# Local attention: probabilities multiplied by their reciprocal sums on GpSimd, statistics later, new orders

## What is computed

```python
def _layer(x, wqkv, qs, ksc, wo, lg, lb, w1, b1, w2, b2):
    h = shift_token(x)                    # half of the channels come from the token before
    q, k, v = split(h @ wqkv)             # 8 heads of 64
    q = l2norm(q) * qs;  k = l2norm(k) * ksc
    q, k = rotary_xpos(q, k)
    o = local_attention(q, k, v)          # windows of 64 tokens, keys of this window and the one before
    x = x + o @ wo
    h = layernorm(shift_token(x)) * lg + lb
    a, g = split(h @ w1 + b1)
    return x + (a * gelu(g)) @ w2 + b2
```

## Time and profile before

| | |
|---|---|
| median of 3 runs | 2002.58 us (1999.52 to 2009.76) |
| the profiled execution | 2001.32 us, its span 1999.5 us |
| mean granted TensorE clock | 0.924 |
| busy: PE, DVE, ACT, POOL | 1614.6, 1371.7, 1116.0, 453.6 us |
| the two pairs | about 614 to 1111 us and 1478 to 1977 us of the span, 32 steps of some 31 us |

### The profile page before, as it was taken

One profiled execution on the slowest core, in us unless ns is written; L12 is line 12 of the kernel. 1 busy time (PEld: TensorE's weight loads), 2 busy tenths in 40 slices (PEclk: granted clock), 3 DMA queues, 4 the chain that ended last, 5 costly groups with the idle time before them and its releaser, 6 DMA issues.

```text
span 1999.5 us, 31315 instructions
## 1 busy us (share of the span) xinstructions
PE 1614.6 (81%) x9756; PEld 1271.6 (64%) x9787; DVE 1371.7 (69%) x3495; ACT 1116.0 (56%) x2975; POOL 453.6 (23%) x342
## 2 busy tenths in 40 slices
PE   6999989666466787888887899999967788888886
PEld 5888887344354565666666687777735666666665
DVE  4678768788956768677786466456656867768673
ACT  2354454332124777778777644434236777777774
POOL 1210010000003334343343100000023334334340
PEclk9999999676678999999999999989979999999998
DMA  4000000000010000000000000000000000000000
GB/s 136 1 1 0 0 0 1 0 1 0 0 53 1 3 3 1 3 2 3 3 1 3 2 1 0 0 0 0 1 0 3 2 3 1 3 3 2 3 1 24
DMA packets 15110, 13.49 MB, mean 7 GB/s; under 512 B 11286, under 2 KB 14266, under 8 KB 14650
## 3 DMA queue, kind: packets, MB, share of 16 engines
q1 hardware_dynamic: 15034, 12.55, 2.0%
HBM read 9.41 MB, written 1.05 MB: 5 GB/s over the span
## 4 chain that ended last, share of the span: by engine, by line
PE 50%; DVE 25%; issue 10%; ACT 7%; DMA 5%; SPq 1%; DVEq 1%; POOL 1%; ACTq 0%; POOLq 0%
DVE prob L1027 5%; DMA HS<-XH 5%; PE bank L1739 4%; PE bank L1680 4%; PE bank L1751 4%; PE bank L1700 3%; PE bank L1879 3%; DVE arena_ffn L984 3%; PE bank L1772 3%; DVE arena_ffn L980 2%; ACT prob L1437 2%; DVE nmaxF L717 2%; PE bank L1883 2%; PE bank L1691 2%; PE bank L1899 2%
## 5 line engine op out<-in xcount | busy, mean ns | idle before, releaser
L556 POOL TENSOR_TENSOR arena_ffn<-arena_ffn 128x1024 f32<-128x1024 f32 x60 | 140.9, 2348 | 434.2 <-DVE arena_ffn L984 434.2
L552 POOL TENSOR_TENSOR inv<-ssq,mhalf 128x16 f32<-128x16 f32 x64 | 188.3, 2942 | 160.6 <-DVE ssq L993 160.6
L1437 ACT ACTIVATE prob<-bank,nmaxF 128x128 f32<-128x128 f32 x512 | 180.9, 372 | 65.7 <-DVE nmaxF L717 65.7
L1751 PE MATMUL bank<-packF,hT 128*128 128x512 f32 x256 | 146.7, 702 | 74.6 <-DVE arena_ffn L984 66.4
L1027 DVE TENSOR_TENSOR prob<-prob,rdenF 128x512 f32<-128x512 f32 x128 | 180.2, 1408 | 4.4
L1714 PEld LDWEIGHTS bank<-arena_setup 128*128 128x128 f32 x1024 | 145.4, 205 | 18.5 <-issue 10.3
L1367 ACT ACTIVATE prob<-bank,nmax 128x128 f32<-128x128 f32 (+1 forms) x256 | 89.9, 420 | 118.3 <-DVE nmax L717 90.5
L1726 PE MATMUL bank<-ident,prob 128*128 128x128 f32 x512 | 83.5, 286 | 79.7 <-DVE prob L1027 79.7
L1714 PE MATMUL bank<-arena_setup 128*128 128x128 f32 x1024 | 143.9, 287 | 0.0
L540 POOL TENSOR_TENSOR rstd<-var,mhalf 128x2 f32<-128x2 f32 x24 | 17.0, 708 | 518.0 <-DVE var L679 518.0
L1726 PEld LDWEIGHTS bank<-ident,prob 128*128 128x128 f32 x512 | 57.1, 144 | 116.8 <-DVE prob L1027 110.0
(11 more groups left out here) (271 smaller groups left out, 4102.4 us busy)
## 6 DMA issues: line engine op xcount, KB each, us to landing
packF<-in_packF SPq DMA_DIRECT2D x1, 3122.0 KB
arena_history<-in_packG SPq DMA_DIRECT2D x1, 2560.0 KB, 9.8
HS<-XH SPq DMA_DIRECT2D x32, 63.5 KB
X<-in_x_tiled SPq DMA_DIRECT2D x1, 1024.0 KB, 5.0
out_dram<-X SPq DMA_DIRECT2D x8, 128.0 KB, 1.9
arena_setup<-in_const_masks_a SPq DMA_DIRECT2D x1, 512.0 KB, 5.5
HS<-XH SPq DMA_DIRECT2D x32, 0.2 KB
arena_setup<-in_const_rope SPq DMA_DIRECT2D x1, 256.0 KB
```

Of the source, the lines that this page charges most:

```text
L552: pool.tensor_tensor(inv[:, t, :, 0], ssq[:, t, :, 0], mhalf[:, 0:16], ALU.pow).then_inc(sems["inv_ready"], 1)
L556: pool.tensor_tensor(t1[:, t], t1[:, t], t2[:, t], ALU.add).then_inc(sems["rope_sum"], 1)
L1437: ins = act.activation(prob[:, u % 2, c * P:(c + 1) * P], bank[u % F_SCORE_BANKS][:, c * P:(c + 1) * P], ACT.Exp, bias=nmaxF[:, u, c:c + 1 ...
L1751: ins = pe.matmul(bank[banks[m]][:], hT[:, t * P:(t + 1) * P], f_at[f"wqkv{l}"][:, 512 * m:512 * m + 512], start=True, stop=True)
```

## The change

The multiplication of the probabilities leaves VectorE and goes to GpSimd; the semaphore "dve_chain" gives way to "rden_ready", which announces each reciprocal. `hidden_stats` goes behind the first two maxima. All four engines get a new order within a step. In the ScalarE and TensorE parts the same calls stand in another order.

```diff
--- before.py
+++ after.py
@@ -120,7 +120,7 @@
     "conv": {"dve_chain": 5, "var_ready": 1, "rstd_ready": 1, "xh_ready": 1,
              "xT_psum": 1, "xT_ready": 1, "down_ready": 1, "down_used": 1},
     "win": {
-        "dve_chain": F_UNITS, "ssq_chain": NT, "stage_ready": 1, "xT_psum": 1, "xT_ready": 1, "qk_psum": NT, "sq_ready": NT,
+        "rden_ready": F_UNITS, "ssq_chain": NT, "stage_ready": 1, "xT_psum": 1, "xT_ready": 1, "qk_psum": NT, "sq_ready": NT,
         "v_psum": NT, "v_ready": NT,
         "ssq_ready": NT, "inv_ready": NT, "rope_ready": NT, "rope_sum": NT, "qk_ready": NT,
         "qkT_psum": NT, "qkT_ready": NT, "s_ready": F_UNITS, "max_ready": F_UNITS, "exp_ready": F_UNITS,
@@ -568,20 +568,37 @@
                     pool.wait_ge(sems["var_ready"], v.at("var_ready", i, 1))
                     pool.tensor_tensor(rstd[:], var[:], mhalf[:, 0:NT], ALU.pow).then_inc(sems["rstd_ready"], 1)
 
+                def weigh(v, i, u):
+                    pool.wait_ge(sems["rden_ready"], v.at("rden_ready", i, u + 1))
+                    pr = prob[:, u % 2].rearrange("p (c k) -> p c k", k=P)
+                    pool.tensor_tensor(pr, pr, rdenF[:, u].broadcast_to([P, 4, P]), ALU.mult).then_inc(sems["norm_ready"], 1)
+
+                def rope_sum(v, i, t):
+                    pool.wait_ge(sems["rope_ready"], v.at("rope_ready", i, t + 1))
+                    pool.tensor_tensor(t1[:, t], t1[:, t], t2[:, t], ALU.add).then_inc(sems["rope_sum"], 1)
+
                 def local_step(n, l, i):
-                    _, nxt, m, hid = around(n, l, i)
+                    v, nxt, m, hid = around(n, l, i)[:4]
                     fin = m and m[0] is vals[n + 3]
                     if nxt:
                         stage_copy(nxt[1], n + 2 * nxt[2])
-                        rope_pool(nxt[0], nxt[1], 0)
+                    weigh(v, i, 0)
                     if hid:
                         hidden_rstd(hid[0], hid[2])
                     if fin:
                         final_add(m[0], m[1])
+                    weigh(v, i, 1)
+                    weigh(v, i, 2)
                     if nxt:
-                        rope_pool(nxt[0], nxt[1], 1)
-                    if fin and m[0] is not vals[-1]:
-                        final_rstd(m[0], m[1])
+                        rope_sum(nxt[0], nxt[1], 0)
+                    weigh(v, i, 3)
+                    if nxt:
+                        inverse_norms(nxt[0], nxt[1], 0)
+                        rope_sum(nxt[0], nxt[1], 1)
+                        inverse_norms(nxt[0], nxt[1], 1)
+                    if fin:
+                        if m[0] is not vals[-1]:
+                            final_rstd(m[0], m[1])
 
                 if kind.startswith("mlp") or kind == "win" and not begins(n):
                     continue
@@ -1014,7 +1031,6 @@
 
                 v, nxt, m, hid = around(n, l, i)
                 fin = m and m[0] is vals[n + 3] and m[0] is not vals[-1]
-                ch = Chain(dve, v, "dve_chain", i)
                 if nxt:
                     vn, ni, nl = nxt
                     sch = Chain(dve, vn, "ssq_chain", ni)
@@ -1022,49 +1038,41 @@
                 def weigh(u):
 
                     dve.wait_ge(sems["exp_ready"], v.at("exp_ready", i, u + 1))
-                    ch.link(dve.reciprocal(rdenF[:, u], denF[:, u]))
-                    pr = prob[:, u % 2].rearrange("p (c k) -> p c k", k=P)
-                    dve.tensor_tensor(pr, pr, rdenF[:, u].broadcast_to([P, 4, P]), ALU.mult).then_inc(sems["norm_ready"], 1)
+                    dve.reciprocal(rdenF[:, u], denF[:, u]).then_inc(sems["rden_ready"], 1)
 
                 scaled(v, i, 1)
+                attn_max(v, i, 0, 4, P, nmaxF, F_SCORE_BANKS)
+                attn_max(v, i, 1, 4, P, nmaxF, F_SCORE_BANKS)
                 if hid:
                     hidden_stats(*hid)
+                weigh(0)
+                if m:
+                    gated(*m)
+                attn_max(v, i, 2, 4, P, nmaxF, F_SCORE_BANKS)
+                weigh(1)
                 if nxt:
                     rope_part(vn, ni, nl, 0, 0)
-                attn_max(v, i, 0, 4, P, nmaxF, F_SCORE_BANKS)
+                weigh(2)
                 if nxt:
                     rope_part(vn, ni, nl, 0, 1)
+                attn_max(v, i, 3, 4, P, nmaxF, F_SCORE_BANKS)
+                if hid:
+                    hidden_apply(*hid)
                 if m:
-                    gated(*m)
-                weigh(0)
-                attn_max(v, i, 1, 4, P, nmaxF, F_SCORE_BANKS)
+                    mlp_end(m[0], m[1])
+                weigh(3)
                 if nxt:
                     norms(vn, ni, 0, sch)
-                attn_max(v, i, 2, 4, P, nmaxF, F_SCORE_BANKS)
-                if nxt:
                     rope_part(vn, ni, nl, 1, 0)
-                weigh(1)
-                attn_max(v, i, 3, 4, P, nmaxF, F_SCORE_BANKS)
-                weigh(2)
-                if m:
-                    mlp_end(m[0], m[1])
-                if nxt:
                     rope_part(vn, ni, nl, 1, 1)
-                weigh(3)
-                if nxt:
+                    scaled(vn, ni, 0)
                     norms(vn, ni, 1, sch)
-                if hid:
-                    hidden_apply(*hid)
-                if nxt:
-                    scaled(vn, ni, 0)
                 if fin:
                     final_stats(m[0], m[1])
+                    norm_apply(m[0], m[1])
                 local_residual(v, i, l)
-                if fin:
-                    norm_apply(m[0], m[1])
                 if nxt:
                     sch.close()
-                ch.close()
 
             def local_residual(v, i, l):
                 dve.wait_ge(sems["down_ready"], v.at("down_ready", i, 1))
@@ -1483,23 +1491,24 @@
                 v, nxt, m, hid = around(n, l, i)
                 if nxt:
                     vn, ni, _ = nxt
-                if nxt:
-                    shifted(vn, ni)
-                    squares(vn, ni, 0)
                 if m:
                     prime(ACT.Gelu)
                     gelus(*m)
                     prime(ACT.Exp, 1)
+                if nxt:
+                    shifted(vn, ni)
                 local_exp(v, i, 0)
                 take_qkT(v, i, 1)
+                local_exp(v, i, 1)
+                if nxt:
+                    squares(vn, ni, 0)
+                local_exp(v, i, 2)
+                middle_values(v, i)
+                probs_copy(v, i, 0)
+                probs_copy(v, i, 1)
+                local_exp(v, i, 3)
                 if nxt:
                     squares(vn, ni, 1)
-                local_exp(v, i, 1)
-                probs_copy(v, i, 0)
-                local_exp(v, i, 2)
-                middle_values(v, i)
-                probs_copy(v, i, 1)
-                local_exp(v, i, 3)
                 take_yT(v, i, 0)
                 probs_copy(v, i, 2)
                 take_yT(v, i, 1)
@@ -1788,36 +1797,33 @@
                 if nxt:
                     vn, ni, nl = nxt
                 pe.wait_ge(sems["v_ready"], v.at("v_ready", i, NT))
-                if nxt:
-                    transpose_x(vn, ni, bank[2])
                 if m:
                     hidden_gates(*m, 0)
-                if nxt:
-                    project_qk(vn, ni, nl, 0)
-                if m:
                     pe.wait_ge(sems["down_used"], v.at("down_used", i, 0))
                     hidden_gates(*m, 1)
                 local_scores(v, i, 0)
                 local_scores(v, i, 1)
+                if nxt:
+                    transpose_x(vn, ni, bank[2])
+                transpose_qk(v, i, 1)
                 if m:
                     hidden_values(*m)
-                transpose_qk(v, i, 1)
+                if nxt:
+                    project_qk(vn, ni, nl, 0)
+                local_scores(v, i, 2)
+                transpose_probs(v, i, 0)
+                local_scores(v, i, 3)
+                if m:
+                    hidden_out(*m)
+                transpose_probs(v, i, 1)
                 if nxt:
                     project_qk(vn, ni, nl, 1)
-                local_scores(v, i, 2)
-                transpose_probs(v, i, 0)
-                if m:
-                    hidden_out(*m)
-                local_scores(v, i, 3)
                 pe.wait_ge(sems["down_used"], v.at("down_used", i, 0))
                 weigh_values(v, i, 0)
-                transpose_probs(v, i, 1)
                 transpose_probs(v, i, 2)
                 if m:
                     pe.wait_ge(sems["m_down_used"], m[0].at("m_down_used", m[1], 1))
                 weigh_values(v, i, 1)
-                if nxt:
-                    project_values(vn, ni, nl, 0)
                 transpose_probs(v, i, 3)
                 weigh_values(v, i, 2)
                 weigh_values(v, i, 3)
@@ -1825,6 +1831,7 @@
                     pe.wait_ge(sems["yT_ready"], v.at("yT_ready", i, 3))
                     transpose_hidden(hid[0], hid[2])
                 if nxt:
```

(1 more changed line is left out.)

## The result

The changed kernel takes 1930.80 us in the median (1930.06 to 1935.67, four runs), the kernel before 2003.38 beside it: a ratio of 0.964, 95% interval 0.961 to 0.967. It is 3.6% faster. The profiled execution took 1935.67, its span 1933.9.

A forecast was written before the change was run, and what follows sets the result against it. No engine is full (TensorE busy 81%), so the order of waits decides. Pairs of -26.4 and -34.9 us, together -61, take 2001.3 to 1940; 0.2 us of missed hops in each of 32 steps gives 1946, range 1912 to 1988.

The forecast's parts named there:

- A: Whole kernel: the forecast itself, 1946 us, by itself 1926 to 1966, chance 0.60.
- The shift: VectorE's wait for the shift DMA, 4.69 us, shrinks to 2.1 behind two maxima; first exponential starts at +4.1.
- The multiplication's price: Four 128x512 multiplies per step on GpSimd: 1.05 us each, ends 1.04 and 1.3; 5.9 us removed from VectorE.
- What is late next: Ordinary step: GpSimd's rotary adds hold VectorE's `hidden_apply` until +14.9, ending +15.8, and `scaled`, ending +24.1.
- The final steps: Batches 2 to 6, second layer: multiplies wait behind `final_add`, TensorE stands 4.3 us; +1.4 first pair, -0.3 second.
- for the clock: Ordinary step: 0.4 us added because TensorE's clock can fall during idleness ahead of the last transposes, making 27.9.
- small hops: All 32 steps: hand-laid orders miss some 0.2 us in each, raising 1940 to 1946.
- the step chosen as a pattern: One stretch between attention residuals, 31.04 us long, read as the ordinary step before the change.
- B: GpSimd's add misses `hidden_apply` and `scaled`; steps come to TensorE's floor, about 25.8 us: 1906, chance 0.12.
- C: Gain half eaten: TensorE waits, then half clock; final steps cost 3 us more each, ordinary 0.5: 1986, chance 0.15.
- D: No gain: table loads and copies on ScalarE still release the first exponential at +9.2: 2000 us, chance 0.06.
- E: Slower: each GpSimd multiply costs as much as the 1024-wide add, 2.35 us: 2035 us, chance 0.07.

The follow-up runs named there:

- the first experiment: The changed kernel with all its new orders, but the multiplication back on VectorE behind each reciprocal: 1955.65 us, 0.974 of the kernel before.

## Why the prediction was right, point by point

The forecast was 1946 in a range of 1912 to 1988; 1930.80 is in it, and in the forecast's own case, A (1926 to 1966), near its fast end. These are rows of the changed kernel's ordinary step, whose first residual ends at 759.53. VectorE:

```profile
761.71 1.51 DVE L734 TENSOR_REDUCE nmaxF<-bank 128x4 f32<-128x512 f32 x2
...
765.60 0.06 DVE L684 MEMSET scratch<- 128x1 f32 x1 [2.39 <-DMA HS<-XH]
...
772.75 1.96 DVE L1104 TENSOR_SCALAR hn<-XH,mv,hrstd 128x64 f32 x1
...
780.13 3.36 DVE L1016 TENSOR_TENSOR arena_attn<-arena_ffn,inv 128x1024 f32<-128x1024 f32 x1 [0.49 <-POOL inv L552]
```

GpSimd:

```profile
772.31 2.35 POOL L578 TENSOR_TENSOR arena_ffn<-arena_ffn 128x1024 f32<-128x1024 f32 x1 [0.20 <-DVE arena_ffn L1001]
...
777.19 2.91 POOL L552 TENSOR_TENSOR inv<-ssq,mhalf 128x16 f32<-128x16 f32 x1 [0.27 <-DVE ssq L1010]
780.07 2.34 POOL L578 TENSOR_TENSOR arena_ffn<-arena_ffn 128x1024 f32<-128x1024 f32 x1
```

TensorE:

```profile
772.29 1.98 PE L1760 MATMUL bank<-packF,hT 128*128 128x512 f32 x4 [0.57 <-DVE arena_ffn L1001]
...
783.55 1.09 PE L1767 MATMUL bank<-ident,arena_attn 128*128 128x128 f32 x8 [1.86 <-DVE arena_attn L1016]
```

- *The shift.* Both maxima run ahead of VectorE's wait for it, and that wait is 2.39, forecast 2.1, before 4.69. The first exponential starts at 763.82, +4.3 against a forecast of +4.1. The runs add its weight: in the old order it brings 76 us alone (2009.64 to 1933.21, the run with only the statistics moved), and without it the rest is a loss.

```profile
763.82 0.37 ACT L1445 ACTIVATE prob<-bank,nmaxF 128x128 f32<-128x128 f32 x1
```

- *The multiplication's price.* 1.041, taken as 1.05 from L520. The GPSIMD Engine Reference of the Trainium skill (introduction and section 3.1) calls elementwise work on GpSimd about twice as slow, which would be an estimated 1.38. The measured 1.04 against an undisturbed 0.69 is 1.5, so the rule is too hard for this shape. For the add of 128x1024 it fits: 2.35 on GpSimd against 1.23 on VectorE, where the run with the second rotary add has it. On the straight line above, 1.38 would still have been a gain; 2.08 was not.
- *What is late next.* `hidden_apply`'s first instruction takes 1.96, and all four end at 775.38, +15.8 as laid out; `scaled` takes 3.36 and ends at 783.49, +24.0 against +24.1. The first instruction of `hidden_apply` ends with GpSimd's add (774.71 and 774.66), and `scaled` ends 1.1 behind the second add (783.49 and 782.41), about its own 1.22 of work. Both are so in all 18 ordinary steps. Moving the second add to VectorE gave back 1.45 of a step, with `scaled` at 1.22, which shows that it was the cost. The page "SBUF — State Buffer" of the Trainium skill (section "SBUF: two separate sides") says that the pair of ports is locked for a whole instruction by whichever starts first. The adds agree, with 3.36 against 1.22; GpSimd's power does not (last section).
- *The ordinary step.* 27.47 measured, 27.5 laid out.
- *The final steps.* 32.41 and 30.91, laid out as 32.7 and 30.4 to 31.0. Here are the rows of GpSimd in a final step of the first pair:

```profile
943.77 0.72 POOL L565 TENSOR_TENSOR X<-X,XH  x1 [5.25 <-DVE XH L1124]
944.45 2.04 POOL L574 TENSOR_TENSOR prob<-prob,rdenF 128x512 f32<-128x512 f32 x2
```

And those of TensorE:

```profile
945.62 1.11 PE L1735 MATMUL bank<-ident,prob 128*128 128x128 f32 x4 [4.52 <-POOL prob L574]
946.53 3.62 PE L1760 MATMUL bank<-packF,hT 128*128 128x512 f32 x4
```

GpSimd stands 5.25 for the MLP's residual with two multiplications behind it, and TensorE 4.52 for them (forecast 4.3). The projection behind that takes 3.62 at a granted clock of 0.50, instead of 1.98 at 1.00. Putting the add last took the wait and the half clock away together, for 1.8 and 2.6 us a step in the mean.

The second pair's number came out by luck in part. The layout let `scaled` wait for the second add there and end at +27.0. But `scaled` started first, as in the first pair, and ended between +25.5 and +26.1 in these five steps. Against that, the projection took 3.3 to 3.6 us at the lower clock, which the layout had not priced, and from its wait to the end of the step TensorE was never idle, so that it was TensorE that set the end. Here are VectorE, GpSimd and TensorE of the step that starts at 1794.17, where TensorE's wait ended at 1810.75:

```profile
1818.50 1.21 DVE L1016 TENSOR_TENSOR arena_attn<-arena_ffn,inv 128x1024 f32<-128x1024 f32 x1
...
1818.66 3.27 POOL L578 TENSOR_TENSOR arena_ffn<-arena_ffn 128x1024 f32<-128x1024 f32 x1 [0.41 <-DVE arena_ffn L1001]
...
1811.49 3.32 PE L1760 MATMUL bank<-packF,hT 128*128 128x512 f32 x4
```

**What was mis-sized.** Against 2001.3, the sum gave -55 and the pairs gave -76. Three terms make nearly all of the 21. The 0.4 us "for the clock" in each ordinary step, 8 us, was not there: the clock stood at 1.00 over the whole step, behind a wait of 1.86 too. (Behind the first experiment's 2.06 it did fall.) The 0.2 us of "small hops" in each of 32 steps, 6 us, was not there either. And the step chosen as a pattern was a little shorter than the mean of before: two in the first pair and one in the second took over 32 (676.73 to 709.46 is one), so that the mean was 31.27 where 31.04 was used, some 4 us; the mean after is 27.37. The stretches outside the pairs then took 10 back in the profiled execution; the median of 1930.80 is 15 under the forecast.

**What the prediction left out.** It laid out the whole change and never asked what each part is worth. The parts don't add up. In the old order the multiplication's move is worth 27 us and the statistics' 76, each against the kernel before in its own comparison, and together with the new orders they are 73; by the pairs alone it is 21, 73 and 76. The table above and the run with only the statistics moved show why: against its 28.9, 29.2 and 23.9 (ordinary, final, last), the whole change has 27.4, 32.4 or 30.9, and 25.3. Over the two pairs that is about -27 us in the ordinary steps, -3 in the opening ones, +24 in the final ones and +3 in the last. Two places pay the gain back: the multiplications behind the final add in GpSimd's queue, 31 us by the run with the add late, and `norm_apply` ahead of the residual, 10 us. With both mended, the multiplication on GpSimd is worth 54 to 61 us. The new orders gain nothing by themselves: with the multiplication on VectorE and the statistics late, the time is 0.974 with them and 0.962 in the old orders (the statistics stand behind two maxima in the one, behind a maximum and both rotary parts in the other). No run has the new orders with neither move.

**The rivals.** B (no conflicts) is out for the ordinary steps, which all had both conflicts; the version without them is at 25.6, near the 25.8 that B gave. In the final steps neither VectorE instruction was held, and it gained nothing there. C (3 more for each final step) is out: the half clock was there, but the steps ended where they had been laid out, in the second pair because `scaled` came sooner than laid out. D is out by the first exponential at +4.3. E is out by the price, and right in its mechanism.

## What to carry to other kernels

Before an operation moves to another engine, list what stands ahead of it in that engine's queue and what that waits for: here an idle engine's four multiplications of 1.04 us cost the ten final steps 1.8 or 2.6 us each and the two last ones 3, through one add with a late input. A wait for a DMA belongs behind what others wait for in its queue and what doesn't need the transfer; that move alone was worth as much as the whole change. And when two parts of a change are costed, run each alone and the pair: gains that share a waiting engine don't add.

## What the runs showed of the hardware

Some of VectorE's instructions are held while GpSimd adds, and a very small one can be. A tensor-scalar of 128x2, 0.17 us before, took 1.58 beside GpSimd's add in the run with only the statistics moved, VectorE first and GpSimd below it:

```profile
740.46 1.58 DVE L1089 TENSOR_SCALAR hvar<-mv 128x2 f32<-128x2 f32 x1
...
739.66 2.35 POOL L556 TENSOR_TENSOR arena_ffn<-arena_ffn 128x1024 f32<-128x1024 f32 x1 [9.25 <-DVE arena_ffn L984]
```

It goes the other way as well. In a final step of the changed kernel `scaled` began 0.17 ahead of the add and took its plain 1.21; the add took 3.27 instead of 2.35, and held the 128x16 tensor-scalar behind it for 1.09 instead of 0.17:

```profile
953.83 1.21 DVE L1016 TENSOR_TENSOR arena_attn<-arena_ffn,inv 128x1024 f32<-128x1024 f32 x1
954.97 1.21 DVE L1009 TENSOR_REDUCE ssq<-arena_attn 128x16 f32<-128x1024 f32 x1
956.21 1.09 DVE L1010 TENSOR_SCALAR ssq<-ssq 128x16 f32<-128x16 f32 x1
...
954.00 3.27 POOL L578 TENSOR_TENSOR arena_ffn<-arena_ffn 128x1024 f32<-128x1024 f32 x1 [0.71 <-DVE arena_ffn L1001]
```

The sum of squares between them, a reduction of 128x1024, took 1.21 beside the same add and was not held.

GpSimd's power did not hold `scaled`, though it too reads two tiles. In the run with only the statistics moved, `scaled` lay wholly inside one and took its plain 1.22:

```profile
756.02 2.91 POOL L552 TENSOR_TENSOR inv<-ssq,mhalf 128x16 f32<-128x16 f32 x1 [1.97 <-DVE ssq L993]
...
756.74 1.22 DVE L999 TENSOR_TENSOR arena_attn<-arena_ffn,inv 128x1024 f32<-128x1024 f32 x1
```

The power reads 16 elements a partition where the add reads 1024 twice; whether that is why was not tested.
